# Sequence stage of an SSM + mixture-of-experts block: scores on 32x64 array tiles, B turned from its copy, states in two array columns, router folded into the output product

## The chip, the cores and the metric

The kernel runs on one core of one Trainium2 chip. The metric is device time in microseconds of one execution. A core has TensorE (PE, with its weight loads PEld), VectorE (DVE), ScalarE (ACT), GpSimd (POOL) and SyncE (SP); each engine takes its own instructions in order, and they wait for each other by semaphores.

## The reference

One block over 2048 tokens of width 128: a state-space layer with 16 heads (head width 8, state size 16, chunks of 64 tokens), a residual and a layer norm, then a layer of 16 experts with the best 4 per token, a residual and a layer norm. Cut to what matters:

```
proj = x @ W_in.T                       # xp, z, B (16x16), C (16x16), dt_low
dt = softplus(dt_low @ dt_W.T + dt_b);  dA = dt * -exp(A_log)
scores = einsum('bcihn,bcjhn->bcijh', C, B) * decay * causal * dt
y_intra = einsum('bcijh,bcjhp->bcihp', scores, xp)
chunk_state = einsum('bckhn,bckhp->bchnp', B, dt * decay_to_end * xp)
h = scan over the 32 chunks: chunk_decay * h + chunk_state
y = y_intra + C h exp(dAcs) + D * xp
y = y / rms(y) * norm_w * silu(z);      x1 = layernorm(x + y @ W_out.T)
logits = -|x1 - key|^2 + x1 @ rw.T + rb;  top 4, softmax of the 4
out = sum over the 4 of gate * (gelu(x1 @ w1.T + b1) @ w2.T + b2)
result = layernorm(x1 + out)
```

## The kernel before, in words

The program has three stages, each written out in order by hand for every engine, in one function.

**Sequence stage.** 16 tiles of 128 tokens, taken in 8 pairs. A loop `for s in range(1, NP)` on PE, DVE and ACT lists calls such as `tile(scores, 2 * s)` (work on one tile) and `pair(residual, s - 2)` (work on one pair); the list is the order of each engine. I call one pass of it a round; round s starts tiles 2s and 2s+1 and finishes the routing of an earlier pair. Per tile PE makes x and B of a tile (`project`, one product of 384 columns), B and C turned (`project_cb`), the scores (`scores`: eight 64x64 products of 256 columns against a block-diagonal copy of C that ACT's `block_diag` builds), the chunk states (`states`), `y_cross`, `y_intra` and `y_back`. DVE masks the scores (`causal0`, `causal1`), scales x (`take_x`) and carries the state over the chunks: `sum0`, `scale0`, `sum1`, `scale1` (`carry_sum`, L949, and `carry_scale`, L958), each needing the one before it. ACT copies B (`take_b`), C and B turned (`cb_copy`) and y (`yiT_copy`).

Per pair: y is scaled and completed (`y_scale`, `y_add`), normed and gated (`gated`), turned (`y_transpose`, `yT_copy`), multiplied by W_out (`out_product`), added to x (`residual`), normed (`res_stats`, `res_moments`, ACT's `log_var` and `inv_dev`, `normed`), turned again (`x2_transpose`, `x2_copy`) and multiplied with the keys (`router`); DVE then finds the best four (`logits`, `best`, `best_ids`, `one_hot`, `chosen`), PE counts the positions (`positions`), and `place`, `slots` and `gates` finish the rows. POOL's `send` writes them: eight indirect transfers per pair, for which `ready` waits.

**Block stage.** 64 full and 8 mixed blocks of rows go through the experts: SP loads a block of rows (`rows_in`), PE turns it (`rows_transpose`) and makes two layers (`hidden`, `expert_out`), DVE copies the expert's weights (`take_w1`), makes row ids and adds the bias, ACT does gelu and the weighing, POOL writes the result rows (`give`). The first 25 blocks (NE) need only the first five pairs (EARLY = 5): SP starts when their rows are sent:

```
            sp.wait_ge(tab_done, 1)
            sp.wait_ge(s1["yi_mm"], NT - 2)
            for k in range(TOPK):
                sp.wait_ge(sent[k], 16 * 2 * EARLY)
```

The last three pairs' routing and sends run beside these blocks. POOL's order is: sends of pairs 0 to 6, `last_root` (the root of the last pair's variance, on which DVE's L1038 of that pair waits), seven result blocks, `last_gates`, then the sends of pair 7 and result blocks in turn. Block 25 waits for the rows of all pairs.

**Final stage.** The sum over four result rows, the last norm and the output.

## Time and profile before

| | |
|---|---|
| Time, median of 3 runs | 315.43 us (315.16 to 316.0) |
| Profiled execution, span | 314.5 us |
| PE busy | 283.4 us (90%) |
| DVE busy | 204.3 us (65%) |
| ACT busy | 209.2 us (67%) |
| POOL busy | 143.7 us (46%) |

The profiled execution's own time is given only as its span; the median lies 0.9 us above it. The start-up takes about 34 us, the sequence stage runs to about 120 us, the block stage from there to about 288 us, the final stage from there to the end. Busy shares are averages over stages with different limits, so each stage is read by itself.

### The profile page before, as it was taken

How to read it: one execution, taken by the hardware profiler on the slowest of the kernel's cores; microseconds unless marked ns; L12 is line 12 of the kernel's file. 1: busy time of each engine (PE TensorE's matmuls, PEld its weight loads, DVE VectorE, ACT ScalarE, POOL GpSimd, SP SyncE). 2: the span in 40 equal slices, each digit the busy share in tenths (PEclk: the TensorE clock that was granted, in tenths of full speed). 3: DMA queues.
4: the chain of work that ended last, by engine and by line, in shares of the span. 5: the costliest groups of instructions: out<-in, count | busy, mean ns of one | idle time of the engine just before them, and what ended most of it. 6: DMA issues, size and time to landing. Idle time of an engine off the chain costs nothing.

```text
span 314.5 us, 10587 instructions
## 1 busy us (share of the span) xinstructions
PE 283.4 (90%) x2948; PEld 250.6 (80%) x2949; DVE 204.3 (65%) x914; ACT 209.2 (67%) x725; POOL 143.7 (46%) x146
## 2 busy tenths in 40 slices
PE   2999899999999997899889899999999999997591
PEld 2986668687677775799779899999999999995480
DVE  2237768898888888866888566555655566641272
ACT  1475466575574743577667688888888889885064
POOL 1200000657456474777677775555555564424000
PEclk9979999999999999599999999999999999999697
DMA  6999920111111111342122232222222222100884
GB/s 212 300 336 374 415 95 2 40 39 57 38 58 48 39 58 47 87 103 78 48 83 90 80 92 72 65 81 71 67 69 67 70 68 60 42 12 6 305 273 92
DMA packets 25260, 33.30 MB, mean 106 GB/s; under 512 B 4299, under 2 KB 18020, under 8 KB 24832
## 3 DMA queue, kind: packets, MB, share of 16 engines
q1 hardware_dynamic: 20432, 23.30, 24.7%
q0 software_dynamic: 4352, 8.79, 7.9%
q10 hardware_dynamic: 432, 0.67, 0.7%
q8 instruction: 22, 0.36, 0.5%
q14 instruction: 22, 0.18, 0.2%
HBM read 21.76 MB, written 11.50 MB: 106 GB/s over the span
## 4 chain that ended last, share of the span: by engine, by line
PE 70%; DVE 11%; DMA 6%; issue 5%; ACT 5%; POOL 1%; DVEq 1%; POOLq 0%; ACTq 0%; SPq 0%
PE bank L774 16%; PE bank L752 15%; PE bank L747 4%; PE bank L539 4%; PE bank L553 4%; DMA yrows<-shared,idi 3%; PE bank L844 3%; PE bank L764 3%; PE bank L530 2%; PE bank L736 2%; PE bank L514 2%; PE bank L591 2%; DMA small<-in_small 2%; PE bank L601 2%; PE bank L563 2%
## 5 line engine op out<-in xcount | busy, mean ns | idle before, releaser
L1881 POOL DMA_INDIRECT yrows<-shared,idi x72 | 75.9, 1054 | 56.1 <-ACT shared L1790 32.6
L1860 POOL DMA_INDIRECT xrows<-rows_all,sli x64 | 62.4, 975 | 81.6 <-issue 63.4
L1769 ACT ACTIVATE shared<-bank,shared 128x128 f32<-128x128 f32 x256 | 73.2, 370 | 19.1 <-PE bank L752 19.1
L752 PE MATMUL bank<-shared 128*128 128x128 f32 x512 | 70.0, 281 | 2.5 <-issue 2.5
L774 PE MATMUL bank<-w2s,shared 128*128 x512 | 68.1, 276 | 0.8 <-DVE shared L1464 0.4
L752 PEld LDWEIGHTS bank<-shared 128*128 128x128 f32 x512 | 63.8, 196 | 3.9 <-issue 3.8
L774 PEld LDWEIGHTS bank<-w2s,shared 128*128 128x128 f32 x512 | 62.3, 192 | 1.4 <-issue 1.4
L1450 DVE COPY shared<-w1s 128x644 f32 x64 | 33.1, 517 | 28.5 <-issue 27.7
L1790 ACT ACTIVATE shared<-shared,idg 128x128 f32<-128x128 f32 x72 | 29.9, 418 | 7.1 <-DVE shared L1464 5.8
L1641 ACT ACTIVATE shared<-bank,small 128x256 f32<-128x256 f32 x64 | 25.1, 476 | 4.7 <-PE bank L539 4.7
L965 DVE TENSOR_TENSOR shared<-bank,small 128x512 f32<-128x512 f32 x32 | 21.2, 682 | 1.3 <-PE bank L553 1.3
L1754 ACT ACTIVATE shared<-bank 128x128 f32<-128x128 f32 x72 | 20.8, 289 | 0.7 <-PE bank L736 0.7
L736 PE MATMUL bank<-cst,shared 128*128 128x128 f32 x72 | 20.5, 284 | 0.0
L1464 DVE TENSOR_TENSOR shared<-bank,shared 128x128 f32<-128x128 f32 x64 | 18.3, 286 | 2.2 <-PE bank L774 1.5
L539 PEld LDWEIGHTS bank<-xT_all,winT 128*128 128x128 f32 x128 | 16.9, 200 | 3.1 <-issue 0.5
L553 PE MATMUL bank<-shared 64*64 64x256 f32 x256 | 18.2, 402 | 0.5 <-issue 0.3
L539 PE MATMUL bank<-xT_all,winT 128*128 128x128 f32 x128 | 18.6, 290 | 0.0
L1429 DVE TENSOR_REDUCE idg<-sel 128x2 f32<-128x8 f32 x72 | 11.6, 161 | 9.6 <-ACT shared L1790 6.7
L1765 ACT ACTIVATE shared<-bank,shared 128x64 f32<-128x64 f32 x64 | 14.0, 329 | 2.4 <-PE bank L747 2.1
L747 PEld LDWEIGHTS bank<-shared 128*128 128x128 f32 x128 | 15.2, 194 | 0.2 <-issue 0.2
L747 PE MATMUL bank<-shared 128*128 128x64 f32 x128 | 15.3, 272 | 0.0
L1422 DVE SCALAR_TENSOR_TENSOR sel<-shared,tb 128x8 f32<-128x8 f32 x64 | 14.0, 219 | 1.8 <-issue 1.7
(221 smaller groups left out, 472.0 us busy)
## 6 DMA issues: line engine op xcount, KB each, us to landing
shared<-xrows SPq DMA_DIRECT2D x64, 70.0 KB
w1s<-in_w1T SPq DMA_DIRECT2D x1, 4128.0 KB, 24.5
w2s<-in_w2T SPq DMA_DIRECT2D x1, 4096.0 KB, 22.9
w1s<-yrows SPq DMA_DIRECT2D x8, 512.0 KB, 7.9
yrows<-shared,idi POOLq DMA_INDIRECT x72
xrows<-zrow SPq DMA_DIRECT2D x1, 1120.0 KB, 13.9
xp_all<-in_xp SPq DMA_DIRECT2D x1, 1024.0 KB, 7.8
w1s<-in_b SPq DMA_DIRECT2D x1, 1024.0 KB, 20.9
```

The source lines that it names most:

```text
L539: m = mm(bank[2][:, k * P:(k + 1) * P], winT[:, c0:c0 + P], xT_all[:, t * P:(t + 1) * P], start=True, stop=True)
L553: m = mm(bank[3 + r][q * Q:(q + 1) * Q, j * 256:(j + 1) * 256], c_[half, 2 + j, q * Q:(q + 1) * Q], cbd[t % 2][half, j, q, :], start=True, ...
L736: pe.transpose(turned_rows(), xb[b.slot(RB)][:, 0:D], ident).then_inc(s3["bt_mm"], 1)
L747: m = mm(hidden_bank(u)[:, f * P + h * HB:f * P + (h + 1) * HB], wh[:, f * P:(f + 1) * P], xbT[u][:, h * HB:(h + 1) * HB], start=True, sto ...
L752: m = mm(hidden_bank(u)[:, f * P:(f + 1) * P], w[:, f * P:(f + 1) * P], xbT[u][:, :], start=True, stop=True)
L774: m = mm(out_bank(u), hT[u][:, f * P:(f + 1) * P], w2s[:, bass.ds(ex, 1), f, :], start=(f == 0), stop=(f == FB - 1))
L1450: ve.tensor_copy(w1c[r][:], w1s[:, bass.ds(expert_of(mybir.EngineType.DVE, b), 1), :].rearrange("p o f -> p (o f)")).then_inc(s3["w1_dve"], 1)
L1641: m = act(cbd[t % 2][:, :, :, h * Q:(h + 1) * Q], bank[2][:, 0:2 * P].rearrange("p (j q i) -> p j q i", j=2, q=NC), cp, scale=sm("head4")[ ...
L1769: m = act(hT[u][:, f * P:(f + 1) * P], hidden_bank(u)[:, f * P:(f + 1) * P], ACT.Gelu, bias=w[:, F + f:F + f + 1])
L1790: act(yw[r][:], yb[u][:], cp, scale=idg[r][:, 1:2]).then_inc(s3["yw_act"], 1)
L1860: po.indirect_dma_start(out=xrows, out_offset=bass.IndirectOffsetOnAxis(ap=sli[:, g, k:k + 1], axis=0), in_=rows_all[:, g, :], in_offset=N ...
L1881: po.indirect_dma_start(out=yrows, out_offset=bass.IndirectOffsetOnAxis(ap=idi[r][:, 0:1], axis=0), in_=yw[r][:, :], in_offset=None, bound ...
```

## The change

- **Scores**: sixteen products of 32 rows x 64 columns with 128 moving columns into four banks, in place of eight 64x64 products of 256; `block_diag` has two instructions in place of four; each `causal` reads half of two banks.
- **B from its copy**: `project` makes only x (128 columns) and turns B twice from ACT's copy `cb`, so it waits for `cb_copy` of its tile.
- **States**: four 64x64 products in two array columns; ACT's new `take_states` copies them, and `carry_sum` reads the copy.
- **Router folded**: W_out @ keys is built once and appended to the output product (144 columns); x @ keys is made with z (144 columns, six groups of z in place of four) and taken by DVE (`take_xk`). `x2_transpose`, `x2_copy` and `router` go; `key_dots`, `key_bias` and `neg_means` come to DVE. The norm (`rows_normed`) and the ids (`ids_packed`) of pairs 0 to 5 move from DVE to ACT.
- **One late bank**: `late` is one bank in place of two; `positions`, `place`, `slots` and `gates` of a pair are done one round later; the skip product goes to bank 5 and waits for the `y_add` before.
- The orders of PE, DVE and ACT are rewritten. EARLY, SP's waits and POOL's order stay.

Cut to its core:

```diff
         def project(t):
...
-                mm(bank[0][:, 0:384], xT_all[:, t * P:(t + 1) * P], winT[:, 0:384], start=True, stop=True
-                   ).then_inc(s1["pj_mm"], 1)
+                pe.wait_ge(s1["cb_act"], t + 1)
+                mm(bank[0][:, 0:D], xT_all[:, t * P:(t + 1) * P], winT[:, 0:D], start=True, stop=True)
...
+                for j in range(2):
+                    m = pe.transpose(bank[0][:, (j + 1) * P:(j + 2) * P], cb[t % 4][:, 2 + j, :], ident)
+                m.then_inc(s1["pj_mm"], 1)
...
             def scores(t):
...
+                pe.wait_ge(s1["s_act"], t + 1)
                 c_ = cb[t % 4]
                 for j in range(2):
                     for q in range(NC):
-                        for r in range(2):
-                            half = slice(r * Q, (r + 1) * Q)
-                            m = mm(bank[3 + r][q * Q:(q + 1) * Q, j * 256:(j + 1) * 256], c_[half, 2 + j, q * Q:(q + 1) * Q],
-                                   cbd[t % 2][half, j, q, :], start=True, stop=True, skip_group_check=True)
+                        for r, b in enumerate(score_banks):
+                            rows = slice(r * HR * NS, (r + 1) * HR * NS)
+                            m = mm(bank[b][q * Q:(q + 1) * Q, j * P:(j + 1) * P], c_[rows, 2 + j, q * Q:(q + 1) * Q],
+                                   cbd[t % 2][rows, j, q, :], start=True, stop=True, skip_group_check=True)
...
             def states(t):
...
-                for j in range(2):
-                    m = mm(bank[7][:, j * P:(j + 1) * P], bs[t % 2][:, j * P:(j + 1) * P],
-                           xz[t % 4][:, j * P:(j + 1) * P], start=True, stop=True)
+                for g in range(4):
+                    j, r = divmod(g, 2)
+                    m = mm(bank[7][r * Q:(r + 1) * Q, 256 + j * Q:256 + (j + 1) * Q], bs[t % 2][:, g * Q:(g + 1) * Q],
+                           xz[t % 4][:, g * Q:(g + 1) * Q], start=True, stop=True, skip_group_check=True)
...
             def skip_products(m_):
...
+                after(s1["y_dve"], m_)
...
+            def take_states(t):
+                ac.wait_ge(s1["st_mm"], t + 1)
+                after(s1["sum_dve"], (t - 1) * NC)
+                act(sS[t % 2].rearrange("p q j (c w) -> p q (j c) w", w=HD),
+                    bank[7][:, 256:384].rearrange("p (jc q w) -> p q jc w", q=NC, w=HD), cp).then_inc(s1["s_act"], 1)
...
             def carry_sum(t, q):
                 if q == 0:
-                    ve.wait_ge(s1["st_mm"], t + 1)
+                    ve.wait_ge(s1["s_act"], t + 1)
...
+            def take_xk(g):
+                n = min(ZG, NT - g * ZG)
+                ve.wait_ge(sil_act, g + 1)
...
         def dt_products(g):
...
-                    pe.wait_ge(sil_act, 4)
+                    pe.wait_ge(xk_dve, NZ)
...
-                pair(gates, s - 2)
+                pair(gates, s - 3)
```

Three places in the orders. First DVE at the end of round 4, before. `yr1` is pair 3, `ge0` pair 2; L998 is `y_add`, L1101 to L1111 are `place` and `slots`, L1118 to L1122 `gates`.

```order
L998 TENSOR_TENSOR yr1<-yr1,bank1 128x256 [waits ys_dve,xd_mm]
L1101 TENSOR_TENSOR pos0<-bank6,cst 128x32 [waits pos_mm]
L1106 TENSOR_TENSOR ohs0<-oh0,pos0 128x128 [waits pl_dve]
L1109 TENSOR_REDUCE slf0<-ohs0 128x8 [waits ohs_dve]
L1111 CAST sli<-slf0 128x8 [waits slf_dve]
L1005 SCALAR_TENSOR_TENSOR yg1<-yr1,rs1,sil_all 128x128 [waits yt_mm,sil_act,rs_act]
L1005 SCALAR_TENSOR_TENSOR yg1<-yr1,rs1,sil_all 128x128
L949 TENSOR_TENSOR st1<-hs1,bank7 128x128 [waits h_dve]
L1118 TENSOR_REDUCE gsum0<-ge0 128x2 [waits ge_act]
L1120 RECIPROCAL gr0<-gsum0 128x2 [waits gsum_dve]
L1122 TENSOR_TENSOR rows_all<-ge0,gr0 128x2x4 [waits gr_dve]
```

After, the end of the same round (`ge1` is pair 1, `yr1` pair 3; L1005 is `y_add` there):

```order
L1140 TENSOR_REDUCE gsum1<-ge1 128x2 [waits ge_act]
L1142 RECIPROCAL gr1<-gsum1 128x2 [waits gsum_dve]
L1144 TENSOR_TENSOR rows_all<-ge1,gr1 128x2x4 [waits gsum_dve]
L1106 TENSOR_REDUCE msk0<-oh0 128x32 [waits pos_mm,oh_dve]
L997 TENSOR_TENSOR yr1<-bank5,fC 128x256 [waits sq_act,y_mm,fC_act]
L1005 TENSOR_TENSOR yr1<-yr1,bank5 128x256 [waits ys_dve,xd_mm]
```

In round s the gates that were those of pair s-2 and stood behind `y_add` are now those of pair s-3 and stand ahead of it. And DVE's start of the next round after:

```order
L955 TENSOR_TENSOR st0<-hs1,shared 128x128 [waits h_dve,s_act]
L964 TENSOR_TENSOR hs1<-st0,gm 128x128 [waits sum_dve,gm_dve,yc_mm]
L955 TENSOR_TENSOR st1<-hs1,shared 128x128 [waits h_dve]
L964 TENSOR_TENSOR hs2<-st1,gm 128x128 [waits sum_dve,gm_dve,yc_mm]
L1117 TENSOR_TENSOR acch<-acc0,msk0 128x16 [waits acc_dve,pos_mm,msk_dve]
L1119 TENSOR_TENSOR acc1<-acch,msk0 128x16 [waits acc1_dve]
L971 TENSOR_TENSOR shared<-bank67,small 128x512 [waits yi_mm,sc_mm]
L1012 SCALAR_TENSOR_TENSOR yg1<-yr1,rs1,sil_all 128x128 [waits yt_mm,sil_act,rs_act]
L1012 SCALAR_TENSOR_TENSOR yg1<-yr1,rs1,sil_all 128x128
L971 TENSOR_TENSOR shared<-bank34,small 128x512 [waits yi_mm,sc_mm]
```

The four state steps (L955, L964) of a tile now stand directly behind each other; before, other work stood between them (L958 and L949 around L990 to L1111 above).

Second PE, the middle of a round, before (L530 is `project`, L636 `x2_transpose`, L563 `states`, L642 `router`, L591 `y_intra`, L539 `project_cb`):

```order
L630 MATMUL bank<-woutn,yT 128x128 x2
L591 MATMUL bank<-shared,xz 16x64 x16
L553 MATMUL bank<-shared 64x256 x8
L530 MATMUL bank<-winT,xT_all 128x384
L636 MATMUL bank<-cst,rows_all 128x128 x2
L563 MATMUL bank<-xz,bs 128x128 x2
L642 MATMUL bank<-kw,x2T 128x16 x2
L591 MATMUL bank<-shared,xz 16x64 x16
L539 MATMUL bank<-xT_all,winT 128x128 x4
```

After (L642 is `y_transpose`, L544 and L548 `project`, L653 `out_product`, L612 `y_intra`, L584 `states`, L557 `project_cb`, L572 `scores`):

```order
L642 MATMUL bank<-cst,yg 128x128 x2
L544 MATMUL bank<-winT,xT_all 128x128
L548 MATMUL bank<-cst,shared 128x128 x2
L653 MATMUL bank<-woutn,yT 128x144 x2
L612 MATMUL bank<-shared,xz 16x64 x16
L584 MATMUL bank<-xz,bs 64x64 x4
L557 MATMUL bank<-xT_all,winT 128x128 x4
L572 MATMUL bank<-shared 64x128 x16
L544 MATMUL bank<-winT,xT_all 128x128
L548 MATMUL bank<-cst,shared 128x128 x2
```

`project` of the even tile stands between the turned y and the output product, `states` and `project_cb` of the odd tile directly behind it.

Third ACT in the middle of a round, before (L1635 is `cb_copy`, L1653 `yiT_copy`, L1681 `log_var`, L1687 `inv_dev`, L1692 `x2_copy`):

```order
L1635 ACTIVATE shared<-bank2 128x512 [waits cbt_mm,sc_mm,yc_mm]
L1653 ACTIVATE yiT0<-bank0 128x256 [waits y_mm,yi_mm]
L1681 ACTIVATE lnv0<-mv0,small 128x2 [waits rv_act,mv_dve]
L1687 ACTIVATE rv0<-lnv0 128x2 [waits xq_dve,x2_dve,lnv_act]
L1692 ACTIVATE x2T0<-bank6 128x256 [waits lg_mm,x2t_mm]
```

After (L1696 is `yiT_copy`, L1671 `take_states`, L1678 `cb_copy`, L1724 `log_var`, L1730 `inv_dev`):

```order
L1696 ACTIVATE yiT0<-bank0 128x256 [waits y_mm,yi_mm]
L1671 ACTIVATE shared<-bank67 128x128 [waits sum_dve,st_mm]
L1678 ACTIVATE shared<-bank2 128x512 [waits cbt_mm,sc_mm,yc_mm]
L1724 ACTIVATE lnv0<-mv0,small 128x2 [waits rv_act,mv_dve]
L1730 ACTIVATE rv0<-lnv0 128x2 [waits x2_act,lg_dve,lnv_act]
```

The variance's log and root now stand behind the copies of the even tile's states and of the odd tile's C and B, which wait for `states` and `project_cb`; before, they stood behind the copy of y.

## Rows read from the trace of the kernel before

**Rows 1.** Windows: length, busy (count) of PE, PEld, DVE, ACT, POOL, granted clock, DMA
```profile
91.22:104.22 13.00, 12.41 (x184) 9.40 (x181) 11.05 (x49) 7.94 (x26) 7.75 (x9) 1.00 0.15 47
128.00:130.00 2.00, 2.00 (x14) 2.00 (x14) 1.76 (x8) 0.58 (x4) 1.70 (x2) 0.50 0.40 114
```

**Rows 2.** Timeline of POOL: start, duration, line, and in brackets the idle time before
```profile
108.16 0.96 POOL L1860 DMA_INDIRECT xrows<-rows_all,sli  x1 [3.05 <-DVE rows_all L1122]
...
117.01 1.05 POOL L1860 DMA_INDIRECT xrows<-rows_all,sli  x1 [0.30 <-issue]
...
121.52 0.96 POOL L1860 DMA_INDIRECT xrows<-rows_all,sli  x1 [3.46 <-DVE rows_all L1122]
...
141.59 0.74 POOL L1887 TENSOR_TENSOR rv<-lnv,cst 128x2 f32<-128x2 f32 x1
```

**Rows 3.** Waits of SP's queue: total, times, longest
```profile
SPq L426 <- DMA xrows<-rows_all,sli: 89.3, 3, 86.8
SPq L446 <- DVE tbi L1226: 3.8, 1, 3.8
```

**Rows 4.** Timeline of PE, the first row of the block stage
```profile
126.75 0.42 PE L736 MATMUL bank<-cst,shared 128*128 128x128 f32 x1
```

**Rows 5.** Timeline of DVE, where the last pair's root arrives
```profile
142.37 0.66 DVE L1038 TENSOR_SCALAR rows_all<-res,mv,rv 128x128 f32<-128x128 f32 x2 [0.86 <-POOL rv L1887]
```

**Rows 6.** Timeline of PE in one round of the sequence stage
```profile
91.22 0.89 PE L530 MATMUL bank<-winT,xT_all 128*128 128x384 f32 x2
91.95 1.05 PE L539 MATMUL bank<-xT_all,winT 128*128 128x128 f32 x8
92.93 1.09 PE L553 MATMUL bank<-shared 64*64 64x256 f32 x16
...
95.86 0.64 PE L591 MATMUL bank<-shared,xz 128*16 128x64 f32 x32
...
98.94 0.44 PE L636 MATMUL bank<-cst,rows_all 128*128 128x128 f32 x2 [0.57 <-DVE rows_all L1038]
99.21 0.61 PE L563 MATMUL bank<-xz,bs 128*128 128x128 f32 x4
99.85 0.62 PE L642 MATMUL bank<-kw,x2T 128*128 128x16 f32 x4
```

**Rows 7.** Timeline of DVE: two state steps in a row, and one round
```profile
28.52 0.29 DVE L949 TENSOR_TENSOR st<-hs,bank 128x128 f32<-128x128 f32 x1
28.91 0.29 DVE L958 TENSOR_TENSOR hs<-st,gm 128x128 f32<-128x128 f32 x1
...
88.29 0.28 DVE L949 TENSOR_TENSOR st<-hs,bank 128x128 f32<-128x128 f32 x1
88.49 0.68 DVE L965 TENSOR_TENSOR shared<-bank,small 128x512 f32<-128x512 f32 x1
...
93.16 0.61 DVE L1005 SCALAR_TENSOR_TENSOR yg<-yr,rs,sil_all 128x128 f32<-128x128 f32 x2 [0.37 <-ACT rs L1671]
...
98.81 0.40 DVE L940 TENSOR_TENSOR xz<-bank,fBz 128x256 f32<-128x256 f32 x1
...
104.27 0.42 DVE L998 TENSOR_TENSOR yr<-yr,bank 128x256 f32<-128x256 f32 x1
```

**Rows 8.** Timeline of ACT in the same round
```profile
94.84 0.38 ACT L1648 ACTIVATE bs<-bank 128x256 f32<-128x256 f32 x1
95.12 0.59 ACT L1635 ACTIVATE shared<-bank 128x512 f32<-128x512 f32 x1
...
97.44 0.29 ACT L1681 ACTIVATE lnv<-mv,small 128x2 f32<-128x2 f32 x1 [0.35 <-DVE mv L1026]
97.77 0.20 ACT L1687 ACTIVATE rv<-lnv 128x2 f32<-128x2 f32 x1
```

**Rows 9.** Timeline of PE: scores of tile 1
```profile
30.21 1.09 PE L553 MATMUL bank<-shared 64*64 64x256 f32 x16
```

**Rows 10.** Timeline of ACT: the third group's exponential
```profile
30.34 0.38 ACT L1624 ACTIVATE gs<-gs 128x208 f32<-128x208 f32 x1 [1.35 <-DVE gs L919]
```

449 lines of the change are left out of this document (244 added, 205 removed).

## Prediction

> **What bounds the kernel now.** I read the windows first, then the timelines of POOL, DVE, PE and ACT in one round, then SP's waits. In the sequence stage a round takes 12.86 us, which is how far apart the same rows of two rounds stand; in a window of one round PE is busy 12.41 us of 13.00 and DVE 11.05 [rows 1]. So PE bounds a round, with DVE less than 2 us behind it. POOL needs eight sends per pair: 108.16 to 117.01 is seven steps of 1.264 us, so 10.1 us for a pair, and it then sits idle 3.46 us until the next pair's rows are ready [rows 2]. The end of the sequence stage is not where the block stage starts. SP waits for the sends of pairs 0 to 4. The last of these is issued at 117.01 and SP's wait for it ends at about 119.5: that is 123.3, where its next wait, 3.8 us for the block table, ends [rows 3], less 3.8, so a send lands 2.5 us after its issue. PE turns the first block at 126.75 [rows 4], 3.4 us after the table. From 121.52 to 141.59 POOL sends pairs 5 and 6 without a gap, then computes the last pair's root [rows 2], for which DVE waits 0.86 us [rows 5]. So behind the round there is a second chain, that of POOL, with 3.46 us of slack ahead of pair 5 and none behind it.
>
> The sum is made against the profiled execution, whose span is 314.5 us; the median of the runs is 0.9 us above, and I add my differences to the median, 315.4.
>
> **PE's own work.** Scores: eight products in 1.03 us (92.93 to the next row at 93.96) [rows 6]. The sixteen new ones are not in the trace. Nearest is `y_intra`, also sixteen products in several array columns: 32 records of 0.018 us, 0.57 us to the next row [rows 6]. From below the bound is 0.57, from above 1.03 (no gain); I use 0.65, near the row that it is most like: 0.4 saved per tile. `project`: 0.73 us (91.22 to 91.95) [rows 6] becomes one product of 128 columns, 0.25 (a quarter of L539's 0.98), and two turns, 0.27 (98.94 to 99.21, L636) [rows 6]: 0.2 saved. `states`: 0.61 for both products [rows 6] becomes some 0.3 (not in the trace; between half, as two columns run together, and no gain): 0.3 saved. `x2_transpose` with its 0.57 us of waiting, and `router` at 0.6, go [rows 6]. Together 2 x 0.9 + 0.27 + 0.57 + 0.6 = 3.2 us per round, less 0.05 for 16 more output columns. PE would need 9.7 us. It stops being the bound.
>
> The Trainium skill weighs in on the scores (TensorEngine Tiling (Array Packing), Key Properties): changing the tiling mode drains TensorE. By TensorE: Matmul & The Clock Gate (LDWEIGHTS), a weight load takes its columns / 1.2 ns whatever its rows, 53 ns for 64 columns; were the 32 loads of a tile one behind the other, an estimate from that page is 1.7 us for a tile's scores. The rows of L553, 16 records at 0.064 us, leave this open.
>
> **DVE.** Two state steps that follow each other directly start 0.39 us apart (28.52, 28.91), while a state step followed by other work frees DVE after 0.20 us (88.29, 88.49) [rows 7]. Put directly behind each other, the four steps of a tile cost about 1.2 in place of 0.8: 0.85 us more per round. Gone to ACT are `normed` (two instructions of 0.66 us together [rows 5], of which I count 0.5, since a following instruction starts before the end) and the ids (0.1); new are `key_dots`, `neg_means` and `key_bias`, 0.4 with one dependence. Reading half of two banks moves as many elements, so `causal` stays at 0.6. 11.05 + 0.85 - 0.6 + 0.4 = 11.7 us: that is DVE's floor for a round (I take 11.6 to 11.7).
>
> **Waits on top of it.** In the new order DVE's work up to the end of `gated` is 2.7 us (steps 1.2, counts 0.3, mask 0.6, gate 0.6). From there a chain runs over three engines: turned y 0.4, `project` of the even tile 0.5 and its tail 0.2, `take_x` 0.4, `take_b` 0.4, `y_intra` 0.6, `states` 0.25, `project_cb` of the odd tile 1.0 and tail 0.2, `cb_copy` 0.5, log 0.3, root 0.2 [rows 6 to 8], and about 0.25 for the semaphores: 5.2. So `square_sums` can start at 7.9. DVE's own work would bring it there at 6.9; the wait is a full 1 us, half of it already at `take_x`, whose x comes 0.5 late. Behind `square_sums` 4.8 us of DVE are left in the round. 2.7 + 5.2 + 4.8 = 12.7 us. So the round goes from 12.86 to 12.7: what was PE's bound becomes DVE's work with two waits in it. ACT has room: 7.94 of 13.00 [rows 1], two fewer `block_diag` instructions per tile, against the state copies and two norms.
>
> **Sends one round later.** This is the step that decides. Before, the gates of pair 4 end round 6: `y_add` of that round starts at 104.27 and ends at 104.7 [rows 7], its first send at 108.16 [rows 2]; the gates lie 0.86 ahead of the send, so 2.6 us behind `y_add`. Counted from the end of round 1 they come at 5 x 12.86 + 2.6 = 66.9. After, they stand in round 7, 1.1 us before its `y_add` ends. Round 2 lacks the work of an earlier pair (12.0), rounds 3 to 6 are 12.7, round 7 also has the table's thirteen small instructions (13.7): 12.0 + 50.8 + 13.7 - 1.1 = 75.4. That is 8.5 us later.
>
> **Start-up.** The key sums, z products of 144 columns and six copies ahead of `dt_products(1)` make about 1.2 us. Scores of tile 1 started at 30.21 [rows 9]; now they wait for `take_states(1)`, which ACT has behind the third group's exponential, 30.34 + 0.38 [rows 10]. 30.72 + 0.3 + 1.2 = 32.2: 2.0 us later. The range is 0 to 3.
>
> **Sum.** The first send of pair 4 moves by 8.5 + 2.0, to 118.7. POOL would feed pair 5 without a gap if it started at 121.52 - 10.1 = 111.4, so the chain of POOL is 7.3 us late, and with it the root at 141.59 and DVE behind it. PE's first block: last send 8.85 us after the first, landing 2.5, load 3.4: 133.4 against 126.75, 6.7 late; the ramp there loses about 1.4 us that `positions`, `gated` and ACT's table load took, but then DVE waits for the root, so 7.3 stands. In the block stage `x2_transpose` and `router` of the last pair are gone and its routing on DVE is spread better: 1.2 us back. The rest (blocks, final stage) is unchanged. 315.4 + 7.3 - 1.2 = 321.5 us.
>
> **The rivals.** *Faster*: the waits don't bind and a round falls to DVE's floor of 11.6. Then the gates of pair 4 come at 10.9 + 46.4 + 12.6 - 1.1 = 68.8, 1.9 us later; with no loss in the start-up POOL is not late at all (110.1 against 111.4), PE's first block comes at 110.1 + 8.85 + 2.5 + 3.4 = 124.8, and with the 1.2 us of the block stage I get 315.4 - 1.9 - 1.2 = 312.3. With 2 us in the start-up it is 314.9. It decides at a mean round of 11.7 us; for it speaks that PE sheds 3 us, against it DVE's 11.05 busy us and its new direct dependences. 0.15. *Same*, a round near 11.8 and some start-up loss: 0.07. *The clock*: at the start of the block stage the granted clock is 0.50 [rows 1], 1.2 GHz, after PE had idled in pieces; in the round it was 1.00, 2.4 GHz, with PE busy 12.41 of 13.00. If PE at 9.7 of 12.7 loses it, its 9.7 us double to 19.4 and six rounds cost 40 us more: about 360. Gaps of PE in the new round are near 1 us. 0.05. *Small tiles don't run together*: scores at twice the old time, 2.05 us per tile, put 1.4 us into the chain of a round in which the odd tile's x waits for the even tile's scores: 14.1, and 7 us more, 328.5. 0.06. By the page's rule on weight loads above it would be this rival; nothing in the rows shows loads of different row groups one after the other. *Forecast*: 0.67.
>
> **Numbers.** 0.3%, 0.95 us, is about what a measurement can tell from no change. The forecast with a round of 12.3 to 13.1 (six rounds of +-0.4) and the start-up's 0 to 3 gives 317 to 326. Slower: 0.67 + 0.05 + 0.06, 0.78; same 0.07; faster 0.15. The range reaches from 314.0, which leaves out most of the faster case, to 328, which leaves out the clock and most of the small tiles.
>
> **What would show it.** In the profile after: POOL's sends without a gap from pair 4 to pair 6, the first of pair 4 near 119; SP waiting for sends, not for the table; PE idle ahead of the first block, at 133; a round of 12.7 with PE busy under 80% of it, DVE waiting for the root (`square_sums`) and for `project` (`take_x`); scores at 0.65 us a tile. Wrong would be: a round under 11.7; POOL with gaps; a granted clock under 1.00 in the rounds.

## The result and the profile after

The change makes the kernel slower: 338.53 us (median of 4 runs, 336.62 to 340.57) against 315.3 (4 runs, 314.5 to 316.0). The ratio is 1.0752, with a 95% interval of 1.0709 to 1.0794. The forecast was 321.5 with a range to 328: the sign is right, and the loss is nearly four times the one forecast. The profiled execution has a span of 338.0 us where before has 314.5. A few executions run over one per cent slower at a lower granted clock: ratios here leave them out, medians and ranges do not, and the profiled execution of e18_no_extra is one.

Read first where the loss has arisen by the end of the sequence stage. Timeline of PE, after (start, duration, line, and in brackets the idle time before):

```profile
150.09 0.44 PE L735 MATMUL bank<-cst,shared 128*128 128x128 f32 x1 [7.09 <-DMA shared<-xrows]
...
169.11 1.44 PE L751 MATMUL bank<-shared 128*128 128x128 f32 x8 [2.02 <-issue]
```

The first block is turned 23.34 us later than in [rows 4], and from there to the end it takes 187.9 us, before 187.75. The whole loss lies ahead of the first block. PE waits 7.09 us for its rows, so the sends decide. (The second row is the longest wait of PE inside the block stage, 2.02 us; e15_both comes back to it.) Timeline of POOL, after:

```profile
104.38 0.96 POOL L1917 DMA_INDIRECT xrows<-rows_all,sli  x1 [5.75 <-DVE rows_all L1144]
...
119.45 0.95 POOL L1917 DMA_INDIRECT xrows<-rows_all,sli  x1 [5.28 <-DVE rows_all L1144]
...
135.45 0.95 POOL L1917 DMA_INDIRECT xrows<-rows_all,sli  x1 [6.21 <-DVE rows_all L1144]
...
145.54 0.96 POOL L1917 DMA_INDIRECT xrows<-rows_all,sli  x1 [0.30 <-issue]
...
165.98 0.74 POOL L1944 TENSOR_TENSOR rv<-lnv,cst 128x2 f32<-128x2 f32 x1
```

Pair 4 is sent from 135.45 on, where it was 108.16 [rows 2]; pairs 5 and 6 and the root follow without a gap. The first sends of two pairs stand 15.1 and 16.0 us apart: the rounds have grown from 12.86 us to some 15.3. One round shows why. Windows of after (length, busy of PE, PEld, DVE, ACT, POOL, granted clock, DMA):

```profile
88.69:104.23 15.54, 12.26 (x223) 9.96 (x215) 11.29 (x49) 7.56 (x25) 7.66 (x8) 0.89 0.12 40
...
88.00:91.00 3.00, 2.62 (x59) 1.99 (x57) 2.56 (x10) 1.79 (x8) 1.85 (x2) 1.00 0.09 29
91.00:93.00 2.00, 0.21 (x2) 0.24 (x3) 1.65 (x5) 0.61 (x2) 1.39 (x3) 1.00 0.18 63
...
95.00:98.00 3.00, 3.00 (x44) 2.69 (x32) 2.02 (x10) 0.66 (x2) 2.24 (x3) 0.50 0.19 64
...
99.00:104.00 5.00, 4.24 (x92) 3.62 (x100) 4.20 (x22) 3.11 (x11) 0.00 (x0) 1.00 0.05 18
```

PE does next to nothing from 91 to 93; then the granted clock is 0.50 from 95 to 98, 1.2 GHz. Window of the next round (PE, clock and DMA only), whose clock falls as well:

```profile
104.23:119.30 15.07, 11.99 (x223) 0.89 0.12 39
```

Timeline of PE in the first of the two:

```profile
90.82 0.17 PE L666 MATMUL bank<-acc,ones 128*128 128x16 bf16 x1
92.79 0.41 PE L642 MATMUL bank<-cst,yg 128*128 128x128 f32 x2 [1.80 <-DVE pos L1123]
...
94.63 1.05 PE L612 MATMUL bank<-shared,xz 128*16 128x64 f32 x32 [0.20 <-ACT bs L1691]
95.61 0.69 PE L584 MATMUL bank<-xz,bs 128*64 128x64 f32 x8
96.23 2.04 PE L557 MATMUL bank<-xT_all,winT 128*128 128x128 f32 x8
98.20 0.69 PE L572 MATMUL bank<-shared 32*64 32x128 f32 x32
```

`y_transpose` (L642) waits 1.80 us for `place` (L1123), and `project_cb` (L557) behind it takes 2.04 us for eight records where `project_cb` took 1.05 before (L539) [rows 6]. Timeline of DVE:

```profile
88.69 0.42 DVE L1005 TENSOR_TENSOR yr<-yr,bank 128x256 f32<-128x256 f32 x1
...
91.28 0.66 DVE L1012 SCALAR_TENSOR_TENSOR yg<-yr,rs,sil_all 128x128 f32<-128x128 f32 x2
91.87 0.68 DVE L971 TENSOR_TENSOR shared<-bank,small 128x512 f32<-128x512 f32 x1
92.47 0.17 DVE L1123 TENSOR_TENSOR pos<-bank,cst 128x32 f32<-128x32 f32 x1
...
99.44 0.16 DVE L1051 SCALAR_TENSOR_TENSOR xq<-mv,rv 128x2 f32<-128x2 f32 x1 [1.31 <-ACT rv L1730]
...
104.23 0.42 DVE L1005 TENSOR_TENSOR yr<-yr,bank 128x256 f32<-128x256 f32 x1
```

`place` (L1123) reads the one late bank that the turn writes, and on DVE it stands behind `gated` (L1012) and behind a mask (L971). This timeline cuts a round into three parts that the experiments can be read by, each from start to start: **head**, `y_add` (L1005) to `y_transpose` (88.69 to 92.79, 4.10); **chain**, from there to `square_sums` (L1051, 99.44, 6.65); **tail**, on to the next `y_add` (104.23, 4.79).

### The profile page after: what moved, and what is told of

Its sections match the earlier page's. It is cut to its first block, busy times and chain, and to the rows that moved or that the text cites. A ratio compares the mean times of both kernels' runs of the same rounds, so it can differ in the third digit from the quotient of the medians.

```text
span 338.0 us, 11210 instructions
## 1 busy us (share of the span) xinstructions
PE 283.2 (84%) x3256; PEld 257.9 (76%) x3257; DVE 208.2 (62%) x926; ACT 205.7 (61%) x721; POOL 144.6 (43%) x146
## 4 chain that ended last, share of the span: by engine, by line
PE 52%; issue 3%; DMA 3%; DVE 3%; ACT 1%; POOL 1%; SPq 1%; POOLq 0%; ACTq 0%; DVEq 0%
PE bank L751 18%; PE bank L773 17%; PE bank L746 4%; PE bank L735 3%; PE bank L763 2%; PE bank L835 2%; PE bank L838 1%; DMA w1s<-yrows 1%; DMA xrows<-rows_all,sli 1%; DMA yrows<-shared,idi 1%; DMA shared<-xrows 1%; PE bank L557 1%; POOL xrows L1917 1%; DVE shared L971 1%; PE bank L612 0%
## 5 line engine op out<-in xcount | busy, mean ns | idle before, releaser
L1938 POOL DMA_INDIRECT yrows<-shared,idi x72 | 77.0, 1070 | 56.6 <-ACT shared L1843 30.4
L751 PEld LDWEIGHTS bank<-shared 128*128 128x128 f32 x512 | 64.6, 198 | 6.9 <-issue 6.6
L773 PE MATMUL bank<-w2s,shared 128*128 x512 | 69.0, 278 | 0.3 <-DVE shared L1489 0.3
L773 PEld LDWEIGHTS bank<-w2s,shared 128*128 128x128 f32 x512 | 63.4, 195 | 0.8 <-issue 0.8
L971 DVE TENSOR_TENSOR shared<-bank,small 128x512 f32<-128x512 f32 x32 | 21.6, 681 | 2.7 <-PE bank L572 2.7
L557 PE MATMUL bank<-xT_all,winT 128*128 128x128 f32 x128 | 22.4, 329 | 0.0
L557 PEld LDWEIGHTS bank<-xT_all,winT 128*128 128x128 f32 x128 | 19.6, 234 | 1.0
L1454 DVE TENSOR_REDUCE idg<-sel 128x2 f32<-128x8 f32 x72 | 11.6, 161 | 9.9 <-ACT shared L1843 7.1
L735 PEld LDWEIGHTS bank<-cst,shared 128*128 128x128 f32 x72 | 10.5, 146 | 8.9 <-issue 8.1
L612 PE MATMUL bank<-shared,xz 128*16 128x64 f32 x512 | 12.3, 248 | 4.4 <-ACT bs L1691 4.3
L1691 ACT ACTIVATE bs<-bank 128x256 f32<-128x256 f32 x16 | 6.1, 383 | 15.7 <-DVE xz L947 15.7
L1678 ACT ACTIVATE shared<-bank 128x512 f32<-128x512 f32 x16 | 9.4, 591 | 10.1 <-PE bank L557 10.1
## 6 DMA issues: line engine op xcount, KB each, us to landing
xrows<-zrow SPq DMA_DIRECT2D x1, 1120.0 KB, 14.1
```

The costliest lines, as they stand in the source:

```text
L557: m = mm(bank[2][:, k * P:(k + 1) * P], winT[:, c0:c0 + P], xT_all[:, t * P:(t + 1) * P], start=True, stop=True)
L735: pe.transpose(turned_rows(), xb[b.slot(RB)][:, 0:D], ident).then_inc(s3["bt_mm"], 1)
L751: m = mm(hidden_bank(u)[:, f * P:(f + 1) * P], w[:, f * P:(f + 1) * P], xbT[u][:, :], start=True, stop=True)
L773: m = mm(out_bank(u), hT[u][:, f * P:(f + 1) * P], w2s[:, bass.ds(ex, 1), f, :], start=(f == 0), stop=(f == FB - 1))
L971: tt(sc[t % 4][:, r * HH:(r + 1) * HH, :].rearrange("p (b h) i -> p b h i", b=2), two_banks.rearrange("p b (h i) -> p b h i", h=H // 4), s ...
L1938: po.indirect_dma_start(out=yrows, out_offset=bass.IndirectOffsetOnAxis(ap=idi[r][:, 0:1], axis=0), in_=yw[r][:, :], in_offset=None, bound ...
```

## The experiments

Three theories are tried. T1: the wait of `y_transpose` for `place` and, behind it, TensorE's clock lengthen the rounds. T2: VectorE's order does, and its wait for the inverse deviation. T3: the sends, one round later, set when the block stage starts. T1 and T2 compete for the rounds; T3 comes on top of either.

The table has medians and ratios from the runs, the rest from one profiled execution each. Each ratio is to runs of the kernel before that were taken together with it (medians 314.96 to 315.7). "`y_add`(0)" is the start of pair 0's `y_add`, "rounds" the mean distance of `y_add` from pair 1 to pair 5, "pair 4" its first send, "block" the start of the first block.

| kernel | median | ratio to before (95%) | `y_add`(0) | rounds | pair 4 | block | span |
|---|---|---|---|---|---|---|---|
| before | 315.3 | | 40.16 | 12.87 | 108.16 | 126.75 | 314.5 |
| after | 338.53 | 1.0752 (1.0709 to 1.0794) | 45.66 | 15.26 | 135.45 | 150.09 | 338.0 |
| e1_place_first | 328.55 | 1.0405 (1.0367 to 1.0444) | 46.27 | 13.58 | 128.23 | 142.66 | 330.2 |
| e2_filler | 332.45 | 1.0512 (1.0447 to 1.0576) | 45.76 | 14.02 | 129.12 | 144.25 | 332.8 |
| e5_project_first | 333.41 | 1.0574 (1.053 to 1.0618) | 45.92 | 14.10 | 129.22 | 143.66 | 331.7 |
| e9_before_wait | 330.1 | 1.048 (1.0442 to 1.0517) | 39.05 | 15.59 | 117.94 | 139.41 | 326.3 |
| e3_gates_early | 329.97 | 1.0448 (1.0415 to 1.0482) | 44.14 | 14.30 | 121.40 | 137.25 | 330.0 |
| e4_before_late_gates | 326.76 | 1.038 (1.0349 to 1.041) | 39.10 | 12.84 | 120.36 | 134.62 | 323.6 |
| e7_place_log | 331.81 | 1.0486 (1.0416 to 1.0557) | 45.90 | 13.58 | 126.78 | 141.32 | 331.6 |
| e8_scores_twice | 337.03 | 1.0671 (1.0634 to 1.0707) | 48.42 | 14.04 | 132.83 | 147.00 | 338.0 |
| e10_gates_early | 323.94 | 1.0291 (1.0255 to 1.0327) | 45.55 | 13.04 | 117.11 | 131.53 | 321.8 |
| e12_start_filler | 322.59 | 1.0214 (1.017 to 1.0257) | 43.93 | 13.03 | 115.45 | 130.42 | 321.4 |
| e14_gated_first | 320.22 | 1.0148 (1.0105 to 1.0191) | 45.50 | 12.43 | 113.65 | 127.89 | 318.0 |
| e15_both | 318.63 | 1.0108 (1.0087 to 1.013) | 43.56 | 12.43 | 111.72 | 126.06 | 316.2 |
| e16b_last_sends | 319.2 | 1.0094 (1.0055 to 1.0133) | 42.65 | 12.42 | 109.23 | 127.31 | 314.2 |
| e17b_start_order | 316.17 | 1.0015 (0.9984 to 1.0045) | 42.43 | 12.44 | 109.09 | 127.51 | 316.1 |
| e18_no_extra | 317.39 | 1.0035 (0.9998 to 1.0072) | 43.11 | 12.43 | 109.81 | 128.95 | 317.7 |

Kernels whose start-up is the same program differ by up to 2 us in `y_add`(0): 44.14 to 46.27 in the eight with that of after (e8_scores_twice left out), 39.05 to 40.16 in the three with that of before.

### The wait and the clock

**e1_place_first**, on the changed kernel:

```diff
+                pair(positions, s - 3)
                 pair(skip_products, s - 1)
...
-                pair(positions, s - 3)
...
                 pair(count_chosen, s - 3)
+                pair(place, s - 3)
                 tile(causal1, 2 * s - 1)
                 pair(gated, s - 2)
                 tile(causal0, 2 * s - 1)
-                pair(place, s - 3)
```

> The changed kernel with positions(s-3) ahead of the skip product on TensorE and place(s-3) right behind count_chosen(s-3) on VectorE, so that y_transpose waits for gated alone. T1 (the one late bank makes y_transpose wait for place, the wait costs about 0.9 us in each of 5 rounds, and the 1.8 us in which TensorE does nothing brings the granted clock to 0.50 for about 4 us behind it, worth another 1.5 to 2 us a round): if the shorter wait (about 1.0 us) still lets the clock fall, -4 us, 334 us with 0.50 windows left; if the clock holds, rounds of 12.7 to 13 us in place of 15.3 and about 326 us. Rival T2 (the rounds are set by VectorE's order and by the inverse deviation behind the second copy of B and C): no change, 338 us, round still 15.3.

Timeline of e1_place_first, PE and then DVE, and its window of the round:

```profile
103.24 0.44 PE L642 MATMUL bank<-cst,yg 128*128 128x128 f32 x2 [1.28 <-DVE yg L1012]
```

```profile
99.88 0.42 DVE L1005 TENSOR_TENSOR yr<-yr,bank 128x256 f32<-128x256 f32 x1
...
108.38 0.16 DVE L1051 SCALAR_TENSOR_TENSOR xq<-mv,rv 128x2 f32<-128x2 f32 x1 [0.43 <-ACT rv L1730]
...
113.18 0.42 DVE L1005 TENSOR_TENSOR yr<-yr,bank 128x256 f32<-128x256 f32 x1
```

```profile
99.88:113.18 13.30, 10.75 (x223) 8.63 (x215) 11.24 (x49) 7.50 (x25) 7.69 (x8) 1.00 0.13 46
```

Head 3.36, chain 5.14, tail 4.80: the head loses 0.74, the chain 1.51, the tail nothing. T1 is borne out and T2 as it was put is not: the 1.31 us that `square_sums` waited were mostly the slow chain. The rounds at the full clock take 13.3 and not the 12.7 to 13 expected, and the total, 328.55, lies between the two numbers expected, for the clock still fell in two rounds of the profiled execution: in that of 72.16 to 86.59, which took 14.43, and in the last (windows, PE, clock and DMA only):

```profile
113.18:128.09 14.91, 11.32 (x221) 0.89 0.13 40
```

**e2_filler** keeps the wait and takes the idleness away:

```diff
                 pair(positions, s - 3)
+                tile(filler, 2 * s)
                 pair(y_transpose, s - 2)
...
+            def filler(t):
+                if t < 6:
+                    return
+                pe.wait_ge(s1["b_act"], t)
+                pe.wait_ge(s1["yit_act"], made["y_intra"])
+                for k in range(5):
+                    mm(bank[0][:, 0:D], xT_all[:, t * P:(t + 1) * P], winT[:, 0:D], start=True, stop=True)
```

> The changed kernel with five extra 128x128 products of x in each round from s = 3 on, ahead of y_transpose, into the place that project(2s) overwrites (they are no part of what is computed): TensorE has work in the gap, and y_transpose waits for place as before. T1: granted clock 1.00 in the whole round, the wait on place 0 to 0.5 us by the rows, rounds 13.3 to 13.8 us in place of 15.3, total 329 to 332 us. Rival (the clock costs nothing, since VectorE sets the round): 338 us or up to 2 us more, by the added work. It tells the price of the clock apart from the price of the wait, which stays.

Window of one round of e2_filler, then its timeline of PE (L557 is the filler there, L650 `y_transpose`):

```profile
86.37:100.43 14.06, 11.98 (x233) 9.78 (x225) 11.30 (x49) 7.54 (x25) 7.66 (x8) 1.00 0.13 44
```

```profile
88.53 1.36 PE L557 MATMUL bank<-winT,xT_all 128*128 128x128 f32 x10
90.48 0.41 PE L650 MATMUL bank<-cst,yg 128*128 128x128 f32 x2 [0.59 <-DVE pos L1132]
```

`square_sums` starts at 95.63, so head 4.11, chain 5.15, tail 4.80. The head is that of after, the chain that of e1. That separates the two prices: the wait for `place` costs 0.75 us a round, the clock 1.5 in the round shown. Over the four rounds from pair 1 to pair 5 the clock costs 15.26 - 14.02 = 1.24 on average: where the clock is already low as the gap ends, as in the rounds of 15.05 and 15.07, the chain takes 6.1 to 6.2 and loses 1.0. The total, 332.45, is just above the 329 to 332 us expected.

**e5_project_first** (`project(2s)` moved ahead of `y_transpose`):

> The changed kernel with project(2s) ahead of y_transpose on TensorE; nothing else moves. take_x(2s) no longer waits behind y_transpose (1.09 us of VectorE per round from s = 3), and 0.65 us of TensorE's work lies in the gap, which leaves 1.2 us idle. T1: -1.1 us a round for the wait of VectorE, 5 rounds: 333 us if the clock still falls; about 326 us if 1.2 us of idleness no longer bring it down. Rival T2: at most -1 us in all, since VectorE then waits for the same copies of ScalarE.

333.41 us, the number expected if the clock still falls, though in the profiled execution it fell in only one of the four rounds (15.22; the others take 13.7 to 13.8 at 1.00). The 1 us at most of T2 is refuted by a gain of 5.1. Why the total isn't nearer the 326 us expected for a clock that holds stays open.

**e9_before_wait** puts the wait into the kernel before:

```diff
             def y_transpose(m_):
                 pe.wait_ge(s1["yg_dve"], m_ + 1)
+                if m_ < NP - 2:
+                    after(s1["acc_dve"], m_)
```

> The kernel before with one wait added: y_transpose(s-2) waits for count_chosen(s-3) as well (pairs 2 to 5), which is done 2.1 us later than y_transpose starts in the trace of before; the computation is whole. T1 (a wait of TensorE of some 2 us costs more than itself, since the clock falls behind it): 0.50 windows behind the wait and rounds of 15.5 to 16.5 us in place of 12.9 in 4 rounds, 326 to 330 us. Rival, the wait alone: at most 2.1 us in each of 4 rounds, up to 324 us with the clock at 1.00 throughout. Rival, the order on VectorE hides it: 316 us.

Timeline of PE and windows of e9_before_wait:

```profile
87.89 0.41 PE L624 MATMUL bank<-cst,yg 128*128 128x128 f32 x2 [2.40 <-DVE acc L1099]
...
90.98 1.99 PE L553 MATMUL bank<-shared 64*64 64x256 f32 x16
```

```profile
82.87:98.92 16.05, 13.62 (x178) 10.07 (x178) 11.16 (x48) 7.74 (x25) 7.66 (x8) 0.89 0.11 38
88.00:91.00 3.00, 3.00 (x57) 2.34 (x56) 0.86 (x3) 1.15 (x3) 2.36 (x3) 0.74 0.20 72
```

The old scores take 1.99 us in place of 1.09 [rows 6]. The round behind this one has the same wait of 2.40 us and keeps the clock (windows, PE, clock and DMA only):

```profile
98.92:114.05 15.13, 12.35 (x178) 1.00 0.13 40
```

Rounds are 15.1 (two, at the full clock, so the wait alone costs 2.2) or 16.1 (two, with the fall, 3.2); a fifth, the last, also has wait and fall. So a wait of one engine for another in the middle of the round costs the kernel before 15.1 us (330.1 against 314.96) with none of the change's other parts; the profiled spans differ by 11.8.

### The sends

**e4_before_late_gates**, one part of the change alone, in the kernel before:

```diff
-                pair(gates, s - 2)
+                pair(gates, s - 3)
...
+            gates(5)
```

> The kernel before with one part of the change alone: gates one round later (gates(s-3) where gates(s-2) stood), so that GpSimd sends the rows of a pair about one round later; the computation is whole. T3 (the sends come one round later, GpSimd then runs through the last pairs without a gap, and the first tokens of the block stage arrive later): first send of pair 4 at 117 us where it was at 108.16, GpSimd's last send some 6 to 9 us later, total +5 to +8 us, 320 to 323 us. Rival (the sends had room, so their lateness is hidden): 315 to 316 us.

Timeline of POOL, then PE, in e4_before_late_gates:

```profile
120.36 0.96 POOL L1861 DMA_INDIRECT xrows<-rows_all,sli  x1 [3.47 <-DVE rows_all L1122]
...
150.91 0.74 POOL L1888 TENSOR_TENSOR rv<-lnv,cst 128x2 f32<-128x2 f32 x1
```

```profile
134.62 0.45 PE L736 MATMUL bank<-cst,shared 128*128 128x128 f32 x1 [7.61 <-DMA shared<-xrows]
```

It costs 11.3 us (326.76 against 315.45), more than the 5 to 8 expected: the send of pair 4 came at 120.36 and not at 117, nearly a full round behind the 108.16 of before. The profiled spans differ by 9.1, and that is POOL's chain: by the prediction it is late by 120.36 - 111.4 = 9.0, and the root came at 150.91, 9.3 later. The first block comes 7.9 us later.

It is the root, more than the first block, that the end goes by. From the root to the end all profiled executions of the table take 171.0 to 174.9 us, with 172.9 before and 172.0 after; from the first block to the end they take 186.9 to 192.8.

**e3_gates_early**, the reverse, in the changed kernel (`gates(s-3)` right behind `slots(s-3)`):

> The changed kernel with gates(s-3) right behind slots(s-3) on VectorE and nothing else; the wait of y_transpose on place stays. T3: the first send of a pair starts about 8 us earlier in its round, the block stage's first token with it, total 338.5 - 8 = 330 to 331 us, rounds unchanged at 15.3. It adds to the gain of e1_place_first, since one shortens the rounds and the other the way from the last round to the first block. Rival (the lateness of the sends is worth only what GpSimd's chain of the last pairs shows, 3 to 4 us): 334 to 335 us.

It gains 8.6 us, as T3 says. Its first send of pair 4 is 14.05 us earlier: 8.7 of these are the place of the gates in the round, 3.85 the shorter rounds, since the clock held in two of the four, and 1.5 the start-up, which is the same program. The root is only 10.5 earlier (155.53 against 165.98), since POOL is no longer fed without a gap: it waits 3.77 us ahead of pair 5. Timeline of PE and windows (PE, clock, DMA only) of two of its rounds:

```profile
75.98 0.41 PE L642 MATMUL bank<-cst,yg 128*128 128x128 f32 x2 [1.75 <-DVE pos L1123]
...
104.29 0.41 PE L642 MATMUL bank<-cst,yg 128*128 128x128 f32 x2 [1.80 <-DVE pos L1123]
```

```profile
71.93:86.52 14.59, 11.94 (x223) 0.88 0.13 41
...
100.19:113.92 13.73, 10.72 (x231) 1.00 0.13 43
```

The same wait brings the clock down in one round and not in another.

### Building the order up again

**e7_place_log** (e1 and `log_var`, `inv_dev` ahead of the second `cb_copy` on ACT; `place` of pair 5 also moves ahead in the tail of the stage, here and in all that follow):

> The kernel with place first (expectation of e1_place_first) and, in addition, log_var and inv_dev ahead of the second cb_copy of a round on ScalarE, so that square_sums on VectorE needs not wait behind the copy. At the full clock that wait is 0.43 us in a round of 13.3 us. T1 with T2 as the rest: rounds 12.85 to 13.0 us, -0.4 us in each of 7 rounds, 325.5 to 326.5 us. Rival (VectorE's own work bounds the round by now, 12.4 us of 13.3, and the copy that comes later makes take_x wait as much): 328.5 us.

A miss: 331.81 us where 325.5 to 326.5 or, by the rival, 328.5 were expected. The wait of `square_sums` is gone, but `take_x` behind it waits some 0.6 us for the `project` that needs the later copy; rounds at the full clock stay at 13.3 us.

**e8_scores_twice** (e1, each product of the scores issued twice in a row):

> The kernel with place first and every product of the scores issued twice (the second overwrites the first with the same numbers): 0.62 us more of TensorE per tile, so the scores cost more than the 64x64 tiles of the kernel before did. If what the small tiles save lies on the path: +1.2 us a round, 337 us. T1 (TensorE no longer bounds the round, VectorE and its chain of waits do; the saving is worth little): +0 to +0.5 us a round, 328 to 332 us. If the added work keeps the granted clock up, it may even be a little faster.

Timeline of PE in e8_scores_twice:

```profile
111.24 1.77 PE L573 MATMUL bank<-shared 32*64 32x128 f32 x64
```

A tile's scores take 1.77 us, 1.08 more and not the 0.62 expected, and the round grows by 0.8 (13.3 to 14.1, both at the full clock) for 2.16 of added work. So TensorE's time is not free in the new round, as T1 had it, nor does it bound it: some 0.37 us for each us. By that the 0.4 us saved per tile are worth 0.3 a round, an estimate. The median grows by 8.5 us to 337.03, the number expected if the saving lay wholly on the path, but not for that reason: in the profiles the first block comes 4.3 later, half of it by the start-up, and the rest lies in the block stage, which has no scores.

**e10_gates_early** (e7 and `gates(s-3)` right behind `slots(s-3)`):

> The kernel of e7_place_log and, in addition, gates(s-3) right behind slots(s-3) on VectorE instead of near the end of the round. The first send of a pair then starts about 7 us earlier within its round. T3: the last send ends 5 to 7 us earlier, and the total is 5 to 7 us below that of e7_place_log, about 320 us. Rival (the sends are no longer what the block stage waits for, y_add of the last pair is): 1 us or less below.

7.9 us less than e7_place_log, a little more than the 5 to 7 expected. The rounds at the full clock are 0.27 shorter each: three small instructions now fill DVE's wait for `project`, which falls from some 0.6 to 0.35, and no longer stand in the tail. One round of e7_place_log also lost 1 us by its clock; no round of e10_gates_early did.

**e12_start_filler** (nine extra products in the start-up), **e14_gated_first** and **e15_both** (both edits), on e10_gates_early. The order of e14:

```diff
                     sum0(2 * s - 1)
+                    pair(place, s - 3)
                     scale0(2 * s - 1)
                     sum1(2 * s - 1)
+                    pair(count_chosen, s - 3)
                     scale1(2 * s - 1)
-                pair(count_chosen, s - 3)
-                pair(place, s - 3)
-                tile(causal1, 2 * s - 1)
                 pair(gated, s - 2)
+                tile(causal1, 2 * s - 1)
```

> The kernel of e10_gates_early with nine extra 128x128 products in the start-up, which are no part of what is computed: four between project_cb(1) and states(0), five between states(1) and scores(1), where TensorE waits for ScalarE. If the start-up is late because TensorE idles and its clock is at half for 13 us in all: clock 1.00 from about 26 us on, y_add(0) 2 to 3.5 us earlier (42 to 43.5 us where it is at 45.55), total 320.5 to 322 us. Rival (the order of ScalarE, take_states ahead of block_diag, sets the start-up): y_add(0) where it was or up to 1 us later, 324 to 325 us.

> The kernel of e10_gates_early with VectorE's work at the head of a round in another order: place and count_chosen between the dependent steps of the state (where each step waits 0.13 us for the one before), gated ahead of causal1. y_transpose then starts about 0.9 us earlier and TensorE's idle time in the gap falls from 1.28 to about 0.4 us. T1: rounds of 12.4 to 12.6 us where they are 13.03, clock 1.00 throughout, 5 rounds: 321 us. Rival (VectorE's work alone bounds the round): 12.8 us, 323 us.

> The edits of e12_start_filler and e14_gated_first together, the best version so far by theory. If both theories hold, 318 to 319 us, still 1% above the kernel before, since the start-up stays 2 us longer and the last rounds are not shortened; if the small tiles and the folded router are worth what they save, under 315 us.

Windows of the start-up, PE, clock and DMA only, in e10_gates_early and then in e12_start_filler:

```profile
20.00:30.00 10.00, 8.49 (x76) 0.50 1.06 382
```

```profile
20.00:30.00 10.00, 9.29 (x109) 0.83 1.05 380
```

`y_add`(0) comes 1.6 us earlier in e12, just short of the 2 to 3.5 expected. That is less than the spread of one start-up from profile to profile, but the three kernels with all nine extra products have it at 42.65 to 43.93, all ahead of the eight without (44.14 to 46.27). In e14 the rounds are 12.4, as expected, below the 12.87 of before: the changed kernel's round can be the shorter one. So VectorE's order was worth 0.6 us a round after all, and that much of T2 holds. In e15 the two add up to 318.63, as expected, and the first block comes at 126.06, ahead of [rows 4]; yet it is 1.1% slower. Timeline of PE and of POOL in e15_both:

```profile
147.71 2.05 PE L759 MATMUL bank<-shared 128*128 128x128 f32 x8 [3.55 <-issue]
```

```profile
124.08 0.95 POOL L1925 DMA_INDIRECT xrows<-rows_all,sli  x1 [2.45 <-DVE rows_all L1152]
144.58 0.74 POOL L1952 TENSOR_TENSOR rv<-lnv,cst 128x2 f32<-128x2 f32 x1
```

The root comes 3 us later than the 141.59 of [rows 2], and PE waits 3.55 us, where no wait at this line was above 0.7 us before. The span is 1.7 us longer: once more the end goes with the root and not with the first block.

**e16_last_sends** (in the last round `slots` and `gates` of pair 4 right behind `gated`, in the tail of the stage those of pair 5 right behind `place`), on e15_both, and **e17_start_order**, on e16_last_sends (with `take_states(1)` ahead of `chunk_decay(2)`, `project(2)` and `take_x(2)` ahead of `scores(1)`, and without five of the nine extra products):

> The kernel of e15_both with slots and gates of pair 4 right behind gated in the last round, and those of pair 5 right behind place in the tail; other pairs stay. In e15_both the first block starts at 126.06 us, earlier than in the kernel before [126.75], yet the block stage takes 190.1 us where before takes 187.8: TensorE waits 3.55 us at 147.7 for the table that comes behind GpSimd's last send (143.5). T3 on the last pairs: pair 5 is sent from 121.5 to 122 us on instead of 124.08, the last send starts at 141 to 141.5, the wait at 147.7 shrinks to 1 to 1.5 us, total -2 us, 316.5 us. Rival (the longer block stage comes from the clock or from the order of blocks): the wait moves but the total stays within 0.5 us of e15_both.

> The kernel of e16_last_sends with the start-up in another order: take_states(1) ahead of chunk_decay(2) on ScalarE (scores(1) waits for it, and it waited 1.5 us behind a factor that VectorE makes late), project(2) and take_x(2) ahead of scores(1), in place of the second group of extra products; four extra products remain. If the start-up is late by these two orders: y_add(0) at 41 to 42 us where it is at 43.56 in e15_both, total -1.5 to -2.5 us, 314 to 315 us, equal to the kernel before or faster. Rival (TensorE falls to half the clock again without the extra products): y_add(0) at 43.5 or later, no gain.

There the kernel before took 388.7 us as well, the two 390.9 and 391.0; nothing is read from these runs. They were run again:

> The kernel of e16_last_sends again, since in that job the kernel before took 388.7 us as well, and its times compare with no other. T3 on the last pairs: pair 5 sent from 121.5 to 122 us on, the wait of 3.55 us at 147.7 shrinks to 1 to 1.5 us, 316.5 us. Rival: within 0.5 us of e15_both (318.6).

> The kernel of e17_start_order again, for the same reason. If the order of the start-up was late: 1 to 2 us below e16b_last_sends, 314.5 to 315.5 us; the disturbed job already showed y_add(0) at 43.07 us against 43.04 for e16, which speaks for the rival, no gain.

> The kernel of e17b_start_order without the four extra products that were left in the start-up: the change with its order alone mended, nothing computed that isn't needed. If the extra products keep the clock up: y_add(0) 1 to 2 us later, total 1 to 2 us more. If they don't matter: the same time as e17b_start_order within 0.5 us.

Timeline of PE in e16b_last_sends:

```profile
146.29 1.13 PE L759 MATMUL bank<-shared 128*128 128x128 f32 x8 [0.79 <-issue]
```

The wait falls from 3.55 to 0.79, as T3 says, but the last round is 1.1 us longer for it and the first block 1.25 later. Its runs lie between 315.72 and 320.17, the profiled one (316.03) is among its fastest, and against e15_both no gain is shown. e17b_start_order is 3 us below e16b_last_sends, yet `y_add`(0) moved by only 0.2 us; where the 3 us come from stays open.

e18_no_extra computes nothing but the changed kernel's work, in the mended order: 317.39, not told apart from before (0.9998 to 1.0072); nor is e17b_start_order (0.9984 to 1.0045), and the 1.2 us between the two lie within the spread of either. It also shows what e17b hides. Windows of the start-up, PE, clock and DMA only, in e14_gated_first and then in e18_no_extra, neither of which has an extra product:

```profile
30.00:40.00 10.00, 7.82 (x127) 0.83 1.05 413
```

```profile
30.00:40.00 10.00, 8.24 (x167) 1.00 1.03 404
```

`y_add`(0) is at 45.50 in the first and at 43.11 in the second: the order alone brings back 2.4 us, about as much as the extra products did in the old order. The two remedies take away the same lateness and don't add up. One profile of each shows this.

No version beat before. What is left of the loss can be read from e17b_start_order: its start-up is 2.3 us longer, its four rounds 1.7 us shorter together, its last round 0.6 us longer, and its first block comes 0.8 later.

## Why the prediction was right in sign and wrong in size

- **The step that failed is "Waits on top of it"**: the round of 2.7 + 5.2 + 4.8 = 12.7, measured 15.26 on average. Chain and tail were right to 0.1 us: 5.14 and 4.80 in e1_place_first, both at the full clock. The head was not 2.7. It took the end of `gated` for the start of the turn, where the order of the changed kernel has the turn wait for `place` as well, behind one more mask. The diff shows `late` as one bank and the wait on `pl_dve` in the turn; I had costed the bank only by the round that it delays the sends. Measured: 0.75 us a round. The head of 3.36 that is left in e1_place_first holds three more things that the 2.7 lacked: `y_add` itself (0.34), state steps of 1.38 in place of 1.2, and 0.1 for `place`.
- **The clock, a rival at 0.05 and one of the signs of being wrong, happened**, though in a milder form than the 360 us that I gave it. I had written that gaps of PE would be near 1 us; with the missed wait it was 1.8, and the clock was at half for somewhat over 3 us in each of the five rounds behind such a gap. It is worth 1.24 us a round on average (e2_filler against after), more than any other term: of the 2.6 us that a round is above the forecast, 0.75 are the wait, some 1.2 the clock and some 0.65 the rest of the head. The missed wait made the gap, and without it the clock held in most rounds, though not in all (e1_place_first).
- **Start-up**, forecast +2.0 with a range to 3, was +5.5: a mis-sized term. PE idles 1.05, 0.46 and 1.25 us there, and the clock is 0.51 from 20 to 30 us where it was 0.83. Either giving PE work there or another order of `take_states(1)`, `project(2)` and `take_x(2)` returns some 2 us (e12_start_filler by 1.6, e18_no_extra by 2.4). What of the other 1 to 2 us is the profiles' own spread, no experiment settled.
- **The sends one round later** were forecast right in kind, and this step alone makes the kernel slower (e4_before_late_gates), so the sign is not luck. POOL had no gap from pair 4 on, SP waited for sends, and PE was idle ahead of the first block. From pair 4's first send to the first block 14.64 us passed, forecast 14.75. The chain of POOL holds too: fed with the send that e4_before_late_gates had, it gives 9.0 where the root came 9.3 later.
- **The sum of what was missed**: pair 4's first send was forecast at 118.7 and came at 135.45, 16.75 us later. The start-up has 3.5 of them, the four rounds from pair 1's `y_add` to pair 5's have 4 x (15.26 - 12.7) = 10.2, the round ahead of them 0.6 and the one behind 2.3. The 1.2 us that the block stage was to give back were counted from the root, and from there 0.9 came back: the root is 24.4 later, the span 23.5. But e9_before_wait, which has none of the change's block stage, shows 1.1 by the same count, so it isn't shown that the change gives them back.
- **Right**: PE no longer bounds the round (10.75 of 13.30 us busy in e1_place_first), and DVE waits for the root (1.31 us at `square_sums`) and for `project` (1.09 at `take_x`). PE's work was put too low, though: its busy time fell from 12.27 us a round (91.41 to 104.27) to 10.75, by 1.5, where 3.2 with a wait of 0.57 in it had been forecast. Scores at 0.65 us a tile came out at 0.62. Timeline of PE in e1_place_first:

```profile
112.59 0.69 PE L572 MATMUL bank<-shared 32*64 32x128 f32 x32
113.21 0.18 PE L663 MATMUL bank<-msk,before 128*128 128x16 bf16 x1
```

- **The rival of small tiles** one behind the other, with 2.05 us a tile, is refuted by these rows, and so is, for 32 loads together, the estimate of 1.7 us that the prediction worked out from the Trainium skill's rate of one load (TensorE: Matmul & The Clock Gate, LDWEIGHTS). The Trainium skill (TensorE: Matmul & The Clock Gate, The mechanism) says that a weight load overlaps with products in flight only when their row groups differ. The trace fits that: four row groups in turn take 0.0216 us per record, and e8_scores_twice, which hits the same place twice in a row, 0.0277. That the weight load is what makes the difference is not shown.
- **DVE's floor** of 11.6 to 11.7 fits the busy 11.24 of e1_place_first only loosely; e15_both, in whose order other work fills the 0.13 us that a state step waits for the one before, has 11.02 busy in 12.52.
- **The range**: with a round of 13.1 and a start-up of 3 the prediction's own sum is 324.9 and not 326. Nothing hangs on it.

## What to carry to other kernels

When two buffers become one, go to each writer and ask which reader of the old content it now waits for, and what stands ahead of that reader on its engine. Here a reader of 0.17 us behind a mask cost 2.0 us a round, wait and clock together, where all products together saved 1.5 us of PE's work. When an engine stops being the bound, look at the length of its idle pieces and not only at their sum: work that it does next may run at half the clock. A step that another engine's chain waits for is priced at the last pair that counts: there, one round later is a whole round.
